# Stage A of a four-stage transformer block: statistics of the heads and the second half of the layer norm taken by ScalarE instead of VectorE

## The reference

```python
x = x + _L0_xattn_ref(_layernorm(x), ctx, ctx, ...)   # stage A: 8 heads of width 32, exponential gates
x = x + _L0_ffn_ref(_layernorm(x), ...)               # stage B: gated FFN, hidden width 768
x = x + _L1_xattn_ref(_layernorm(x), ctx, mask, ...)  # stage C: attention with softmax
x = x + _L1_ffn_ref(_layernorm(x), ...)               # stage D: FFN 1024, two GELU layers
```

```python
log_f = jax.nn.log_sigmoid(fg);  cs = jnp.cumsum(log_f, axis=1)
log_D = where(mask, cs[:, :, None] - cs[:, None, :], -inf) + ig[:, None, :]
D_mat = jnp.exp(log_D - max_log_D);  C = qk * D_mat
normalizer = jnp.maximum(jnp.abs(C.sum(axis=-1, keepdims=True)), jnp.exp(-max_log_D))
h = jnp.einsum('hst,htd->hsd', C / (normalizer + EPS), vh)      # then put together to 256 columns
mu = h.mean(axis=-1, keepdims=True);  var = h.var(axis=-1, keepdims=True)
return (h - mu) / jnp.sqrt(var + LN_EPS) * ln_scale
```

## Time and profile before

| | |
|---|---|
| median of the runs | 613.81 us (611.12 to 615.84) |
| the profiled execution | 609.11 us, span 607.3 us, mean granted TensorE clock 0.961 of full speed |
| TensorE matmul | 550.9 us busy, 91% of the span |
| VectorE | 347.0 us busy, 57% |
| ScalarE | 213.8 us busy, 35% |
| GpSimd | 76.4 us busy, 13% |
| chain of work that ended last | PE 69%, DVE 4%, issue 2%, ACT 1% |

### The profile page before, as it was taken

The page is one execution under the profiler, slowest core; times in us unless marked ns, Lnnn a source line. Parts: engine busy times, 40 slices in busy tenths (PEclk is TensorE's granted clock), DMA queues, the critical chain, the costliest instruction groups (busy, mean ns, idle before and its releaser), DMA issues.

```text
span 607.3 us, 8958 instructions
## 1 busy us (share of the span) xinstructions
PE 550.9 (91%) x2728; PEld 448.5 (74%) x2728; DVE 347.0 (57%) x853; ACT 213.8 (35%) x372; POOL 76.4 (13%) x104
## 2 busy tenths in 40 slices
PE   3297988978999999879999999999899999999994
PEld 2165666666888887757888888888778888888884
DVE  6568899878777868856243454353363434542232
ACT  2223332244668744237212244112261122441220
POOL 4213142116000023300000010000100000000001
PEclk9689989777999999979999999999999999999999
DMA  7666544538854859710000000000100000000000
GB/s 192 140 165 154 120 112 74 156 113 296 320 188 136 178 189 263 157 36 1 1 0 2 0 36 1 0 2 0 38 1 1 0 1 9 27 1 0 1 0 36
DMA packets 57762, 47.73 MB, mean 79 GB/s; under 512 B 37278, under 2 KB 48542, under 8 KB 57316
## 3 DMA queue, kind: packets, MB, share of 16 engines
q1 hardware_dynamic: 51960, 28.29, 18.2%
q0 software_dynamic: 5616, 18.88, 9.6%
q10 hardware_dynamic: 148, 0.04, 0.0%
HBM read 40.58 MB, written 2.10 MB: 70 GB/s over the span
## 4 chain that ended last, share of the span: by engine, by line
PE 69%; DVE 4%; issue 2%; ACT 1%; POOL 0%; DVEq 0%; ACTq 0%; POOLq 0%
PE ps L800 52%; PE ps L569 5%; PE ps L570 5%; PE ps L557 2%; DVE xn L1102 1%; PE ps L771 1%; PE ps L563 1%; PE ps L565 1%; PE ps L564 1%; ACT al L1030 1%; PE ps L785 1%; ACT h L1065 0%; DVE sc L1350 0%; DVE x L1321 0%; ACT kr L1017 0%
## 5 line engine op out<-in xcount | busy, mean ns | idle before, releaser
L800 PE MATMUL ps<-hBt,h 128*128 128x512 f32 x512 | 117.5, 390 | 0.0
L800 PE MATMUL ps<-hA,h 128*128 128x512 f32 x512 | 117.2, 390 | 0.0
L800 PEld LDWEIGHTS ps<-hA,h 128*128 128x128 f32 x512 | 95.9, 188 | 20.2 <-DVE hA L1396 0.4
L800 PEld LDWEIGHTS ps<-hBt,h 128*128 128x128 f32 x512 | 95.8, 188 | 20.2 <-DVE hBt L1396 0.4
L1065 ACT ACTIVATE h<-ps,scol 128x512 f32<-128x512 f32 x64 | 44.2, 690 | 175.4 <-PE ps L800 175.3
L800 PE MATMUL ps<-xT,w 128*128 128x512 f32 x256 | 60.3, 395 | 1.9 <-issue 1.9
L800 PEld LDWEIGHTS ps<-xT,w 128*128 128x128 f32 x256 | 46.5, 189 | 15.2 <-issue 2.8
L1411 DVE CAST hBt<-h 128x512 fp32r<-128x512 f32 x32 | 13.7, 427 | 73.7 <-ACT h L1065 73.7
L1411 DVE CAST hA<-h 128x512 fp32r<-128x512 f32 x32 | 13.7, 427 | 70.1 <-ACT h L1065 70.1
L416 POOL TENSOR_TENSOR rstd<-ve,mhalf 128x4 f32<-128x4 f32 x16 | 16.4, 1025 | 253.9 <-DVE ve L1097 253.9
L569 PE MATMUL ps<-xT,l 128*128 128x512 f32 x96 | 40.3, 420 | 5.0 <-DVE hfB L1309 2.8
(11 more groups left out here) (168 smaller groups left out, 900.7 us busy)
## 6 DMA issues: line engine op xcount, KB each, us to landing
looked<-w_all_in SPq DMA_DIRECT2D x16, 704.0 KB, 4.8
h<-w_all_in POOLq DMA_DIRECT2D x16, 512.0 KB, 6.3
V<-ctx_in SPq DMA_DIRECT2D x32, 128.0 KB, 4.5
Qb<-xT SPq DMA_DIRECT2D x64, 64.0 KB, 2.1
w<-w_all_in POOLq DMA_DIRECT2D x3, 1024.0 KB, 6.9
x<-x_in SPq DMA_DIRECT2D x4, 512.0 KB, 4.6
kstA<-ctxT_in SPq DMA_DIRECT2D x4, 512.0 KB, 5.4
kstC<-ctxT_in SPq DMA_DIRECT2D x4, 512.0 KB, 5.9
```

The source lines that it names most:

```text
L800: last = mm(o, a, b, start=(k == 0 and p == 0), stop=(k == n_k - 1 and p == 1))
```

## The change

ScalarE takes over two things in stage A's loop. `head_stats` reads hm twice, with an accumulated output: the first pass gives minus the mean (`hnm`), the second the sum of squares of h minus mean (`hss`). GpSimd adds 256e-5 (`epsD`) and takes the power -0.5; the missing factor of 16 is multiplied into `lns` once, before the loop. `x_norm` becomes four activations with scale `rstd` and bias `nmr`, the latter a small new VectorE instruction (`x_shift`). VectorE drops `bn_stats`, `bn_aggr` and the addition behind each hm, and the four instructions of `x_norm` inside the loop (the two calls ahead of the loop stay). A sign change in `gate_b` is folded into the instruction ahead of it.

```diff
+            step(nc.gpsimd.memset(epsD[:, :], 1e-5 * D))
             settle()
             inv_root(0)
...
             def h_root(b, par):
                 pool.wait_ge(s["hstat_ready"], b + 1)
+                nc.gpsimd.tensor_tensor(hve[:, par:par + 1], hss[:, par:par + 1], epsD[:, 0:1], ALU.add)\
+                    .then_inc(s["hve_ready"], 1)
+                pool.wait_ge(s["hve_ready"], b + 1)
                 nc.gpsimd.tensor_tensor(hrs[:, par:par + 1], hve[:, par:par + 1], mhalf[:, 0:1], ALU.pow)\
...
+            def x_norm(n, b0):
+
+                act.wait_ge(s["nmr_ready"], n - 1)
+                for q in range(Q):
+                    last = fn(xn[:, q, :], x[:, b0 + q, :], ACT.Identity, scale=rstd[:, q:q + 1],
+                              bias=nmr[:, q:q + 1])
+                last.then_inc(s["xn_ready"], 1)
+
+            def head_stats(b, par):
+                act.wait_ge(s["pv_used"], b + 2)
+                flat = hm[:, par, :, :].rearrange("p h d -> p (h d)")
+                fn(spill[:, :], flat, ACT.Copy, scale=-1.0 / D, accum_out=hnm[:, par:par + 1])\
+                    .then_inc(s["hnm_ready"], 1)
+                act.wait_ge(s["hnm_ready"], b + 1)
+                fn(spill[:, :], flat, ACT.Square, bias=hnm[:, par:par + 1], accum_out=hss[:, par:par + 1])\
+                    .then_inc(s["hstat_ready"], 1)
...
                         if k == 3:
+                            if u == 0:
+                                with act.If(i > 0):
+                                    head_stats(2 * Q - 1, 1)
+                            else:
+                                head_stats(Q * g - 1, 1)
                             more(lambda: log_part(gn))
                         if k == 4:
+                            head_stats(Q * g, 0)
                             more(lambda: floor_part(gn))
+                        if k == 6:
+                            if u == 0:
+                                x_norm(g + 2, 8 - 8 * i)
+                            else:
+                                more(lambda: x_norm(3, 3 * Q))
                         if k == UN - 1:
-
-                            act.wait_ge(s["raw_here"], g + 1)
+                            head_stats(Q * g + 1, 1)
+                            act.wait_ge(s["hi_ld"], 64 * (g + 1))
...
                                 more(lambda: x_hi(3, u))
+                            head_stats(Q * g + 2, 0)
             act.wait_ge(s["raw_seen"], G + G // 2)
             fn(facc[:, 0:2 * G], facc[:, 0:2 * G], ACT.Copy, accum_out=fsum[:, 0:1]).then_inc(s["flag_sums"], 1)
...
+            head_stats(NB - 1, 1)
             table_set(SILU)
             act.wait_ge(s["xA_done"], NB)
...
+            def x_shift(n):
+                dve.wait_ge(s["rstd_ready"], n + 1)
+                v.scalar_tensor_tensor(out=nmr[:, :], in0=mv[:, :, 0], scalar=-1.0, in1=rstd[:, :],
+                                       op0=ALU.mult, op1=ALU.mult).then_inc(s["nmr_ready"], 1)
...
-                ch.step(v.scalar_tensor_tensor(out=Z[:, 1, :], in0=gi[:, :], scalar=gb[:, 0:1], in1=cs[:, :],
-                                               op0=ALU.add, op1=ALU.subtract))
-                ch.settle()
-                ch.step(v.tensor_scalar(Z[:, 1, :], Z[:, 1, :], -1.0, None, ALU.mult))
+                ch.step(v.scalar_tensor_tensor(out=Z[:, 1, :], in0=cs[:, :], scalar=gb[:, 0:1], in1=gi[:, :],
+                                               op0=ALU.subtract, op1=ALU.subtract))
...
-                dve.wait_ge(s["pv_used"], b + 2)
-                ch.step(v.bn_stats(h6[:, :], flat))
-                ch.settle_apart()
-                ch.step(v.bn_aggr(hmv[:, q % 2, :], h6[:, :]))
-                ch.settle()
-                v.tensor_scalar(hve[:, q % 2:q % 2 + 1], hmv[:, q % 2, 1:2], 1e-5, None, ALU.add)\
-                    .then_inc(s["hstat_ready"], 1)
                 ch.end()
...
+            v.tensor_scalar(lns[:, :], lns[:, :], float(D) ** 0.5, None, ALU.mult).then_inc(s["lns_ready"], 1)
             ch = gate_a(0)
...
                         if q == 2:
+                            if u == 0:
+                                x_shift(g + 2)
+                            else:
+                                more(lambda: x_shift(3))
                             more(lambda: gate_c(gn, state["ch"]))
                             more(lambda: floor_copy(gn, 1 - u))
                             finish(b - 1, u, q - 1, norm=True)
-                            if u == 0:
-                                x_norm(g + 2, 8 - 8 * i)
-                            else:
-                                more(lambda: x_norm(3, 3 * Q))
```

More of the change, by code:

```diff
@@ L137, in two_layers @@
         mhalf = place(base, "mhalf", [P, Q], F32)
-        h6 = place(base, "h6", [P, 6], F32)
-        hmv = place(base, "hmv", [P, 2, 2], F32)
+        nmr = place(base, "nmr", [P, Q], F32)
+        hnm = place(base, "hnm", [P, 2], F32)
+        hss = place(base, "hss", [P, 2], F32)
+        epsD = place(base, "epsD", [P, 1], F32)
         hve = place(base, "hve", [P, 2], F32)
@@ L166, in two_layers @@
         looked = [place(lows_at, f"looked{m}", [P, FLAG_W], F32) for m in range(FLAG_BUFS - 1)]
+        spill = place(lows_at, "spill", [P, D], F32)
         looked.append(place([w_end - 6 * HD], f"looked{FLAG_BUFS - 1}", [P, FLAG_W], F32))
@@ L226, in two_layers @@
         names = """x_first x_second x_rest ident_ld gw_ld consts mask_ld mask_free hi_ld
-            raw_here raw_seen gw_lo gw_cast const_set mv_ready rstd_ready xn_ready tr_done xhi_done xlo_done x_free
+            raw_seen nmr_ready hnm_ready hve_ready lns_ready gw_lo gw_cast const_set mv_ready rstd_ready xn_ready tr_done xhi_done xlo_done x_free
             khi_done klo_done gate_done gate_copied gate_moved ab_ready ln_ready ncs_ready er_ready z_ready
@@ L484, in _ @@
                     pool.wait_ge(s["hi_ld"], 64 * (g + 1))
-                    pool.sem_inc(s["raw_here"], 1)
                     if u == 0:
@@ L671, in _ @@
             pv(NB - 1, 1, 2, Q - 1)
-            pe.wait_ge(s["raw_here"], G)
+            pe.wait_ge(s["hi_ld"], 64 * G)
             pe.wait_ge(s["c_ready"], UN * G + 2)
@@ L1115, in k_lo @@
                     .then_inc(s["klo_done"], 1)
-            A2 = 9
+            A2 = 8
             def gate_a(g):
@@ L1174, in centre @@
                 h = hm[:, par, :, :].rearrange("p h d -> p (h d)")
+                dve.wait_ge(s["lns_ready"], 1)
                 dve.wait_ge(s["hrs_ready"], b + 1)
-                v.scalar_tensor_tensor(out=h, in0=h, scalar=hmv[:, par, 0:1], in1=lns[:, :],
-                                       op0=ALU.subtract, op1=ALU.mult).then_inc(s["centred"], 1)
+                v.scalar_tensor_tensor(out=h, in0=h, scalar=hnm[:, par:par + 1], in1=lns[:, :],
+                                       op0=ALU.add, op1=ALU.mult).then_inc(s["centred"], 1)
             def add_on(b, par):
@@ L1194, in finish @@
                     centre(b - 1, (q - 1) % 2)
-                ch = Chain(dve, s["dve_unit"], 7, b)
+                ch = Chain(dve, s["dve_unit"], 4, b)
                 pvb = ps[:, PV:PV + 2, 0:Q * PVW].rearrange("p a (j w) -> p a j w", j=Q)
                 floor = ET[:, par, :].rearrange("p (j a q) -> p a j q", a=2, q=Q)[:, :, :, q]
-                flat = hm[:, q % 2, :, :].rearrange("p h d -> p (h d)")
                 dve.wait_ge(s["pv_done"], b + 3)
```

## The result

The changed kernel takes 615.42 us (median, 610.54 to 622.09); the kernel before took 612.67 us in the same rounds (607.56 to 616.99). The ratio is 1.0061, 95% interval 1.0031 to 1.0091: slower by 1.9 to 5.6 us. It is not the quotient of the two medians, which is 1.0045 (2.75 us). The forecast was 615.2 us, 1.4 over before, and no change above 1%. The sign and the class are right; the size is 1.4 us short by the medians and 2.3 by the ratio's 3.7 us. That 615.2 lies only 0.2 from the measured median is luck: the forecast stood on a median of 613.81 us for the kernel before, which came out 1.1 us lower in these rounds.

A forecast was written before the change was run, and what follows sets the result against it. TensorE's waits, with SyncE's queue beside them, were taken to bound the loop, not VectorE's load. Terms -0.25 - 0.3 - 1.15 + 3.1 = +1.4 us on a median of 613.8 gave 615.2, range 609.5 to 621.0.

The forecast's parts named there:

- What bounds the loop: Stage A's loop: TensorE's waits count; nearly all of some 19 us taken off VectorE is cover, not path.
- Rival (1): Stage A's loop: VectorE was the bound; the loop gives 8.4 us, the end takes 3.1, so 608.5; chance 0.14.
- my case: Whole kernel: the author's own forecast, +1.4 us, groups 1 and 2 at 25.9 and 24.8 us; chance 0.64.
- The 0.25 us ahead of the loop: Ahead of the loop: gate_b is on the path and loses its sign change, -0.25 us.
- SyncE's queue: Ends of groups 0 to 2: queued DMAs limit how early zp moves; terms 0, -0.3 and -1.15 us.
- the cap: End of group 2: VectorE's 1.5 us gain is cut to the 1.22 SyncE's queue allows; -1.15 us taken.
- the forecast sign: End of group 1: zp's move would still follow the Qb DMAs without a gap.
- Group 3: Group 3: no gates or x_norm, TensorE sets the pace until the last exponential, VectorE's slack worth nothing: 0.
- End of the loop: Sequences 13 to 15: ScalarE's passes and flag sum delay the last pv 2.6 us, statistics of 15 add 0.5: +3.1.
- Rival (2): Each group's sixth exponential: ScalarE's order becomes the bound, passes waiting for hm hold it up; 622.9 us, chance 0.14.
- Rival (3): End of the loop: free because group 3's sequences run ahead, only the gains stay; 612.1 us, chance 0.08.
- Prices: Instruction costs: ScalarE's pair of passes 1.2 us, x_norm 2.0, GpSimd's addition 0.24; VectorE loses some 19.

The follow-up runs named there:

- end on VectorE: Changed kernel with the heads' statistics of sequences 6, 14 and 15 back on VectorE; ratio to the kernel before 1.0005 (0.9972 to 1.0038).
- x_norm alone, values last: Kernel before with x's normalisation on ScalarE, folded sign, and SyncE's values DMAs behind zp's move and the queries; ratio 0.9997.
- Heads alone: Changed kernel with the normalisation of x back on VectorE, heads' statistics staying on ScalarE; ratio to the kernel before 1.014, measured again 1.009.
- x_norm alone, again: Second measurement of the kernel before with x's normalisation on ScalarE and the sign folded, heads left on VectorE; ratio 0.9985.
- before, values last: Kernel before with SyncE's four DMAs of the next group's values behind zp's move and the queries; ratio 1.002.
- values last: Changed kernel with SyncE's four DMAs of the next group's values behind zp's move and the queries; ratio to the kernel before 1.0072.

## Why the prediction was right

**What bounds the loop: right.** VectorE's load was cover. The change took some 16 us off it; groups 0 to 2 lasted 79.94 and 79.39 us where they lasted 80.38, 0.4 to 1.0 less, against 1.45 forecast (0.3 and 1.15 for groups 1 and 2). Rival (1), 8.4 us from the loop, is dead: group 1 lasts 25.80 and group 2 24.33, against "25.9 and 24.8" for my case and 23.5 for the rival. But the spread of groups 0 to 2 between two traces of one code is 3.8 and 8.2 us, so the agreement of the terms inside it is not shown. That there is no gain of 8 us is shown by the timed runs, since the end costs only some 3. The 0.25 us ahead of the loop cannot be seen either: the loop starts at 27.88 us before, and at 28.85 and 27.46 in the two traces of the change.

**SyncE's queue: half right.** In group 2 the cap was as described. The queue gets through its queries at 103.37 and issues Rr at 103.42, though zp had been written at 102.98. In group 1 the forecast sign failed: the queue was free at 78.69, and the move waited for zp (written 79.22, moved 79.24). Group 0 ended on the queue as forecast (zp written at 48.18, queue free at 49.58), but the pause of TensorE was 5.54 us where it had been 2.3. What I had not drawn is the other side of the cap:

```profile
107.62 6.45 SPq L290 DMA_DIRECT2D Qb<-xT  x8
108.79 0.38 PE L606 MATMUL ps<-Rr,Lr 15*128 15x512 bf16 x1 [0.88 <-DMA Lr<-zp]
116.94 0.50 PE L569 MATMUL ps<-Qb,kT 128*128 128x512 f32 x1 [3.03 <-DMA Qb<-xT]
```

These are SyncE and TensorE at the start of group 3 with the change. Before it was

```profile
106.28 11.76 SPq L287 DMA_DIRECT2D Qb<-xT  x9
108.26 0.60 PE L600 MATMUL ps<-Rr,Lr 15*128 15x512 bf16 x1
```

The queries behind the move had 1.98 us on the group's start, now 1.17: TensorE meets them sooner. It waits 3.03 us for the second block of queries (2.93 in the second trace), and in the 5.5 us behind that wait the granted clock is 0.69 in both.

**Group 3: wrong by the traces, the step that failed.** I put 0 to it. Counted from the group's start (108.26 before, 108.79 with the change), its fifth expo came at 10.85 us before and comes at 13.65 (13.26 in the second trace):

```profile
119.11 0.39 PE L600 MATMUL ps<-Rr,Lr 15*128 15x512 bf16 x1
122.44 0.38 PE L606 MATMUL ps<-Rr,Lr 15*128 15x512 bf16 x1
```

That is 2.4 to 2.8 us, behind the Qb pause and the half clock after it. In "end on VectorE" the pause was 2.15, the clock of the group 1.00, and the fifth expo at 10.93, with the statistics of sequences 7 to 12 on ScalarE as in the change; "x_norm alone, values last" has the heads on VectorE and loses 3.1 us in the same place. So this loss goes with the landing and the clock, not with the passes themselves. "Heads alone" has no Qb pause and reaches the last pv 1.8 us sooner than the change (24.38 against 26.21), but it is not faster in the runs. How often the loss happens in the executions that nobody traced, and so how much of the measured 2.8 to 4.0 us it makes up, is not known.

**End of the loop: right, in mechanism and nearly in size.** From the fifth expo to the start of the heads of 14: 9.94 us before, 10.60 with the change, so 0.7 for a forecast 0.9. From those heads out to the last pv: 0.06 us before (heads out at 129.47, pv 129.53), 1.54 now (133.46 to 135.00), so 1.5 for 1.2 + 0.4 + 0.1 - 0.1 = 1.6.

```profile
129.05 0.42 DVE L1211 TENSOR_TENSOR hm<-ps,den 128x256 f32<-128x256 f32 x1
```

Behind the last pv 18.13 for 17.35, 0.8 for 0.5. Sum 2.9, forecast 3.1. The last of the three is the unsure one. In the trace of before the last pv ran at a granted clock of 0.55 and took 3.44 us; in the four other traces with the heads on VectorE and the end unchanged it took 2.03 to 2.29, and the stretch behind it 15.95 to 16.20. Against these the change loses 1.9 to 2.2 there, so the term may be mis-sized by up to 1.7 us. Group 3 and the end grew by 5.4 to 5.7 together, since the 2.4 to 2.8 of group 3 stand ahead. That the order at the end costs time, and is not merely a part that moved, rests first on its addition to the kernel before (1.0056, with only 0.2 us lost ahead of the fifth expo). Its removal from the change (1.0005) agrees, but that trace had lost nothing in group 3 either. Setting the flag's product behind the pv, which takes 2.1 us off the traced end, left 1.0059, and this does not fit well. So the end is a cause that is shown, and that it is the whole cost is not.

**Rival (2), ScalarE's order: not seen at this load, real at the next.** The sixth exponential of group 3 is the place named, and it shows:

```profile
124.52 0.51 ACT L921 ACTIVATE spill<-hm,hnm 128x256 f32<-128x256 f32 x1
125.03 0.57 ACT L975 ACTIVATE Dt<-ps 128x512 f32<-128x512 f32 x1
125.80 0.69 DVE L1206 SCALAR_TENSOR_TENSOR Ct<-ps,Dt 128x512 f32<-128x512 f32 x1 [1.14 <-ACT Dt L975]
```

It costs one late multiplication and no chain of them. The row that I gave for this rival, a last pv of 3.44 us after a wait of 1.08, does not repeat:

```profile
129.20 2.20 PE L624 MATMUL ps<-V,CtB 128*128 128x99 f32 x16 [1.18 <-DVE hm L1228]
```

That is the same pv in "x_norm alone, again". **Rival (3)** is refused by the facc wait and by the run with the passes added to before.

**Prices.** A pass took 415 and 508 ns, with the mean of 462 ns near the straight line's 0.49; the pair with its reads is 0.42 + 0.19 + 0.51 + 0.19 less overlap, 1.14 us measured from 81.16 to 82.30, for 1.2. x_norm on ScalarE took 2.06 us in four, for 2.0, though one of its activations lasts 589 ns and not 490: they overlap. The addition on GpSimd took 0.189, for 0.24. VectorE lost 16.3 us of the 19: the difference is mostly the semaphore gaps that I had counted as work, 0.98 us a sequence from hm's end to hve's end, of which only 0.76 (0.43, 0.18, 0.15) are busy time.

**What stays open.** The two traced executions differ by 9.9 us: 1.0 ahead of the loop, -0.4 in groups 0 to 2, 5.7 in group 3 and the end, and 3.6 in what follows. This last part, the rest of the program, code-identical, took 464.1 and 464.0 us with the change and 460.4 before. One group of the page holds 2.7 us of it, in the changed kernel

```profile
L806 PE MATMUL ps<-xT,w 128*128 128x512 f32 x256 | 61.9, 403 | 3.0 <-issue 3.0
```

for 60.3 us, 395 ns and 1.9 us of idle time before. At the seam between stages C and D TensorE also runs longer at half clock. In three stretches of 5 us from 268.13 on the granted clock is 0.78, 0.50 and 0.70; at the same work before (from 261.88) it was 0.61, 0.71 and 1.00. Other variants with the heads on ScalarE have 460.1 to 462.8, so it isn't the heads as such. I did not find what sets it, and the medians (+3 to +4 us) say that it isn't there in every execution, or that the single trace of before, 609.11 us against medians of 611 to 614, was a good one.

## What to carry to other kernels

Read an engine's fullness only together with the waits: 16 us taken from an engine as busy as TensorE gave nothing that could be measured. In the traces the starts of the groups hung on DMAs and on the order in which they are issued; opening that order alone gave nothing either. Where work is moved to another in-order engine, look for the place at which that engine answers to somebody (here a sum that lets the last matmuls go): steady work in the loop showed no cost, and the last two or three items, with nothing left to hide them, cost some 3 us by the trace and 1.6 to 5.2 by the runs. Move the loop's share and leave the last items where their latency is shortest. And a group that ends sooner meets the transfers behind it sooner.

## What the hardware showed that I had not expected

- The same code, traced twice, differs by 3.8 us over three groups (80.90 and 84.71), and in another case by 8.2 (87.69 and 79.48), while the piece from the fifth expo to the last pv repeats to 0.00 to 0.04 us. Where a group waits for a DMA, one trace tells the mechanism and not the size.
- A pause can cost twice, and its length does not say whether. After 5.54 us for Lr the expo matmul takes 0.60 us in place of 0.38; after 4.10 us, in "end on VectorE", it took 0.38 and the next one 0.60. After 3.54 us for facc the last 16 pv matmuls take 3.73 us, where those of sequence 14 took 1.92; after 1.08 us they took 3.44 in one trace (before) and 2.21 in another (before, values last). When the pause for Lr was taken out (values last), the time did not follow.
- Each pointer operand lengthens an activation of 256 columns by some 90 ns: 415 ns with constant scale, 508 with a bias pointer, 589 with scale and bias pointers. Activations that follow each other overlap, so four of the last kind take 2.06 us (77.90 to 79.96), 0.51 each.
- GpSimd adds 128x1 in 0.189 us but raises 128x1 to a power in 0.573, so a second small instruction there is cheap beside the first.
